# Second attention: exponentials over 1536 columns out of two score buffers of three banks, sums of every seventh tile on ScalarE

## What is computed

```python
q, k, v = jnp.split(x_proj, 3, axis=-1)
att = jnp.einsum('blhd,bmhd->blmh', q, k) * scale
att = jax.nn.softmax(att, axis=2)
opt = jnp.einsum('blmh,blhd->blhd', att, v).reshape(b, l, d)
...
x = x + _L1_attn_ref(xn, ...) + _L1_ffn_ref(xn, ...)   # second layer
```

## Time and profile before

| | |
|---|---|
| Time, median of 3 runs | 1465.37 us (1465.34 to 1466.09) |
| Time of the profiled execution | 1468.72 us |
| Its span, first to last instruction | 1467.0 us |
| ScalarE busy | 1428.0 us |
| VectorE busy | 1220.8 us |
| TensorE busy | 1110.7 us |
| GpSimd busy | 884.5 us |
| First exponential of the second attention | 975.7 us |

### The profile page before, as it was taken

The page is one execution under the profiler, slowest core; times in us unless marked ns, Lnnn a source line. Parts: engine busy times, 40 slices in busy tenths (PEclk is TensorE's granted clock), DMA queues, the critical chain, the costliest instruction groups (busy, mean ns, idle before and its releaser), DMA issues.

```text
span 1467.0 us, 22437 instructions
## 1 busy us (share of the span) xinstructions
PE 1110.7 (76%) x8231; PEld 445.9 (30%) x8260; DVE 1220.8 (83%) x2196; ACT 1428.0 (97%) x796; POOL 884.5 (60%) x656
## 2 busy tenths in 40 slices
PE   5587787888788888888887675777777677776766
PEld 2133224245143352452542311322223122221212
DVE  6998889978879879789788588838898898998886
ACT  3999999999999999999999999989999999999998
POOL 5188998878789898898898985933213023022100
PEclk8599988999999999899999897889999999999999
DMA  4942544222322235254353231034033033021020
GB/s 121 253 141 65 167 129 125 60 61 73 82 82 62 64 102 155 80 144 131 83 155 96 69 75 31 13 120 81 27 128 71 27 113 81 27 106 33 23 70 20
DMA packets 113185, 130.04 MB, mean 89 GB/s; under 512 B 42906, under 2 KB 81178, under 8 KB 113066
## 3 DMA queue, kind: packets, MB, share of 16 engines
q1 hardware_dynamic: 107738, 116.74, 29.5%
q0 software_dynamic: 4464, 11.09, 2.8%
q10 hardware_dynamic: 864, 0.69, 0.2%
HBM read 83.79 MB, written 44.70 MB: 88 GB/s over the span
## 4 chain that ended last, share of the span: by engine, by line
ACT 38%; POOL 27%; DVE 15%; issue 12%; PE 6%; DMA 2%; SPq 1%; ACTq 0%; DVEq 0%; POOLq 0%
ACT exp L1352 13%; ACT scores L830 11%; ACT scores L791 6%; DVE exp L1360 6%; DVE scores L737 6%; POOL scratch L775 3%; POOL scores L773 3%; ACT exp L1348 3%; PE pvb L718 3%; POOL gate L1098 3%; POOL scratch L784 3%; POOL scores L786 3%; POOL scratch L780 3%; ACT h L1091 2%; POOL scratch L777 1%
## 5 line engine op out<-in xcount | busy, mean ns | idle before, releaser
L737 DVE TENSOR_SCALAR scores<-ring 128x1024 f32<-128x1024 f32 x512 | 591.8, 1216 | 62.2 <-PE ring L703 58.9
L830 ACT ACTIVATE scores<-scores 128x8192 f32<-128x8192 f32 x63 | 438.9, 7020 | 0.2
L1352 ACT ACTIVATE exp<-ring 128x1024 f32<-128x1024 f32 x438 | 431.4, 1388 | 4.4 <-PE ring L1327 3.9
L718 PE MATMUL pvb<-scores,val 128*9 128x256 f32 x4096 | 338.3, 406 | 97.8 <-ACT scores L830 63.7
L1327 PE MATMUL ring<-stk 128*128 128x512 bf16 x995 | 300.9, 386 | 131.2 <-ACT exp L1352 103.4
L791 ACT ACTIVATE scores<-scores 128x7296 f32<-128x7296 f32 (+2 forms) x59 | 384.1, 6574 | 4.9 <-DVE scores L737 4.8
L1360 DVE SCALAR_TENSOR_TENSOR exp<-exp 128x512 f32<-128x512 f32 x438 | 322.3, 758 | 62.6 <-ACT exp L1352 55.6
L703 PE MATMUL ring<-stk 64*128 64x512 bf16 x1024 | 216.1, 419 | 59.2 <-DVE scores L737 45.4
L1327 PEld LDWEIGHTS ring<-stk 128*128 128x128 bf16 x1024 | 66.1, 97 | 341.7 <-ACT exp L1352 232.5
L703 PEld LDWEIGHTS ring<-stk 64*128 64x128 bf16 x1024 | 50.0, 94 | 303.4 <-DVE scores L737 182.3
L718 PEld LDWEIGHTS pvb<-scores,val 128*9 128x9 f32 x4096 | 65.8, 89 | 226.9 <-issue 223.5
(11 more groups left out here) (263 smaller groups left out, 1434.9 us busy)
## 6 DMA issues: line engine op xcount, KB each, us to landing
stk<-stack SPq DMA_DIRECT2D x192, 192.0 KB, 2.8
w<-in_w SPq DMA_DIRECT2D x39, 352.0 KB, 3.6
w<-in_w SPq DMA_DIRECT2D x39, 192.0 KB, 2.7
stack<-qp SPq DMA_DIRECT2D x7, 768.0 KB, 4.4
stack<-kp SPq DMA_DIRECT2D x7, 768.0 KB, 5.4
xj<-xg SPq DMA_DIRECT2D x10, 448.0 KB
yg<-xj POOLq DMA_DIRECT2D x10, 448.0 KB, 3.6
stack<-qp SPq DMA_DIRECT2D x7, 512.0 KB, 5.1
```

What stands on the lines that cost most here:

```text
L718: mm = nc.tensor.matmul(pvb[place % 2][32 * c:32 * c + VW, 0:256], val[place][:, j, :], S[place][:, j * N + c * 256:j * N + (c + 1) * 256] ...
L737: nc.vector.tensor_scalar(S[place][:, j * N:(j + 1) * N], tile, 1e-12, None, ALU.max).then_inc(o.release(("qk", group, place, j)), 1)
L830: nc.scalar.activation(S[place][:], S[place][:], ACT.Exp, scale=-1.0).then_inc(exp_done, 1)
L1352: nc.scalar.activation(EX[k // 2][:, k % 2, :], tile, ACT.Exp, scale=SCALE1).then_inc(o.release(("qk1", n, i)), 1)
```

## The change

Scores go into two buffers of three banks, `wide0` and `wide1`, which take the place of `ring0` to `ring2` for the second attention; `widen` makes TensorE wait for all three old buffers first. Half tiles of 512 columns are counted through, and a span is a run of three of them (`SPAN_HALVES` = 3, 3, 3, 3, 2): four spans of one and a half tiles and one of a single tile, which holds tile 6 of a round of 7. That tile is summed on ScalarE in the first three batches; in the last batch VectorE sums all but the last 8 tiles. The first 504 tiles are cut in this way, the last 8 stay single. TensorE makes three matmuls for a wide span, ScalarE one exponential of 1536 columns; VectorE's sums remain one for each tile. `EX` is one tensor of 14 tiles used round and round, and the wait for the sums becomes one for each span, 14 tiles back. Because it is larger, the first exponential waits for the products of S[1] too. The auxiliary work stays at its steps; a span is filled at the step of its first tile, two spans ahead.

```diff
 def sum_by_act(n, i):
-    s = n % H * NT + i
-    return n < HEADS - H and 12 <= s < 124 and s % 5 == 1 or n >= HEADS - GROUP and i >= LAST_PARTS[-1][0]
+    return n < HEADS - H and (n * NT + i) % SPAN_TILES == SPAN_TILES - 1 or n >= HEADS - GROUP and i >= LAST_PARTS[-1][0]
...
+SPAN_HALVES, TILE_HALVES = (3, 3, 3, 3, 2), 2
+SPAN_TILES = sum(SPAN_HALVES) // TILE_HALVES
+EXP_TILES = 14
+LAST_SPANS = HEADS * NT - GROUP * (LAST_PARTS[-1][1] - LAST_PARTS[-1][0])
...
+for span_halves in LAST_SPANS // SPAN_TILES * SPAN_HALVES + (HEADS * NT - LAST_SPANS) * (TILE_HALVES,):
+    SPANS.append(range(len(SPAN_OF), len(SPAN_OF) + span_halves))
+    SPAN_OF.extend(span_halves * [len(SPANS) - 1])
...
+    def widen(self, pe, tiles):
+
+        for slot in range(RING):
+            pe.wait_ge(self.free[slot], self.turn[slot])
+        self.tiles, self.slot, self.slots = [*tiles, *self.tiles[len(tiles):]], 0, len(tiles)
...
-            EX = [late_room(f"exp{i}", [P, 2, N]) for i in range(NT // 2)]
+            EX = late_room("exp", [P, EXP_TILES * N])
...
+        with ExitStack() as own:
+            wide = [psum(own, f"wide{i}", [P, 3 * 512]) for i in range(2)]
...
+        def pe_scores1(pe, o, span):
+            tile = o.begin(pe, ("exp", span))
+            for k, half in enumerate(SPANS[span]):
+                (n, i), cols = tile_of(half), HALVES[half % TILE_HALVES]
+                if i == 0 and half % TILE_HALVES == 0:
+                    pe.wait_ge(stk1_in[n % GROUP], 16 * (n // GROUP + 1))
+                mm = nc.tensor.matmul(tile[:, k * 512:(k + 1) * 512], stk1[n % GROUP][:, Q, i * P:(i + 1) * P],
+                                      stk1[n % GROUP][:, K, cols], start=True, stop=True)
+            mm.then_inc(ring_full, 1)
+
+        def act_exp1(act, o, span):
+            halves = SPANS[span]
+            (n, i), last = tile_of(halves[0]), halves[-1] // TILE_HALVES
+            tile = o.filled(act, ("exp", span))
+            if span == 0:
+                act.wait_ge(pv_done, CHG * (GROUPS - 1) + 2 * CH)
+            if last >= EXP_TILES and FOLDS[last - EXP_TILES + 1]:
+                act.wait_ge(summed, FOLDS[last - EXP_TILES + 1])
...
         def dve_fold(dve, o, b, s):
-            (n, i), k = tile_at(b, s), s % NT
-            o.emptied(dve, ("qk1", n, i))
+            (n, i), half = tile_at(b, s), (b * H * NT + s) * TILE_HALVES
+            o.emptied(dve, ("exp", SPAN_OF[half + 1]))
...
-                for i in range(RING):
-                    pe_scores1(pe, o, 0, i)
+                o.widen(pe, [tile[:] for tile in wide])
+                made = len(wide)
+                for span in range(made):
+                    pe_scores1(pe, o, span)
...
-                        if b or s >= RING:
-                            pe_scores1(pe, o, *tile_at(b, s))
+                        while made < len(SPANS) and SPANS[made][0] // TILE_HALVES <= b * H * NT + s:
+                            pe_scores1(pe, o, made)
+                            made += 1
```

More of the change, by code:

```diff
@@ L205, in begin @@
         if slot is None:
-            slot, self.slot = self.slot, (self.slot + 1) % RING
+            slot, self.slot = self.slot, (self.slot + 1) % self.slots
         if self.turn[slot]:
@@ L210, in begin @@
         self.made[kind], self.turn[slot] = self.made[kind] + 1, self.turn[slot] + 1
-        self.of[key] = (kind, self.made[kind], slot, self.turn[slot])
+        self.of[key] = (kind, self.made[kind], slot, self.turn[slot], self.tiles[slot])
         return self.tiles[slot]
+    def widen(self, pe, tiles):
+        for slot in range(RING):
+            pe.wait_ge(self.free[slot], self.turn[slot])
+        self.tiles, self.slot, self.slots = [*tiles, *self.tiles[len(tiles):]], 0, len(tiles)
     def fills(self, key):
@@ L217, in filled @@
     def filled(self, eng, key):
-        kind, made, slot, _ = self.of[key]
+        kind, made, _, _, tile = self.of[key]
         eng.wait_ge(self.full[kind], made)
-        return self.tiles[slot]
+        return tile
     def release(self, key):
@@ L225, in emptied @@
     def emptied(self, eng, key):
-        _, _, slot, turn = self.of[key]
+        _, _, slot, turn, _ = self.of[key]
         eng.wait_ge(self.free[slot], turn)
@@ L1329, in scores1, with tile_of @@
             return mm
-        def pe_scores1(pe, o, n, i):
-            if i == 0:
-                pe.wait_ge(stk1_in[n % GROUP], 16 * (n // GROUP + 1))
-            tile = o.begin(pe, ("qk1", n, i))
-            scores1(tile, n % GROUP, i).then_inc(ring_full, 1)
-        def act_exp1(act, o, b, s):
-            (n, i), k = tile_at(b, s), s % NT
-            tile = o.filled(act, ("qk1", n, i))
-            if n:
-                if k % 2 == 0:
-                    act.wait_ge(summed, FOLDS[b * H * NT + s - NT + 2])
-            elif i == 0:
-                act.wait_ge(pv_done, CHG * (GROUPS - 1) + CH)
-            if sum_by_act(n, i):
+        def tile_of(half):
+            return tile_at(*divmod(half // TILE_HALVES, H * NT))
@@ new lines, in exp_cols @@
+        def exp_cols(half):
+            return half % (EXP_TILES * TILE_HALVES) * 512
+        def pe_scores1(pe, o, span):
[7 more added lines that the diff above has]
+            mm.then_inc(ring_full, 1)
@@ new lines, in act_exp1 @@
+        def act_exp1(act, o, span):
[6 more added lines that the diff above has]
+                act.wait_ge(summed, FOLDS[last - EXP_TILES + 1])
+            at_col = exp_cols(halves[0])
+            out, tile = EX[:, at_col:at_col + 512 * len(halves)], tile[:, 0:512 * len(halves)]
+            if len(halves) == TILE_HALVES and sum_by_act(n, i):
@@ L1346, in act_exp1 @@
                 if n >= 2 * GROUP:
                     act.wait_ge(w_done, n // GROUP - 1)
-                nc.scalar.activation(EX[k // 2][:, k % 2, :], tile, ACT.Exp, scale=SCALE1,
+                nc.scalar.activation(out, tile, ACT.Exp, scale=SCALE1,
                                      accum_out=den[n // GROUP % 2][:, n % GROUP, i:i + 1]
-                                     ).then_inc(o.release(("qk1", n, i)), 1)
+                                     ).then_inc(o.release(("exp", span)), 1)
@@ L1351, in act_exp1 @@
             else:
-                nc.scalar.activation(EX[k // 2][:, k % 2, :], tile, ACT.Exp, scale=SCALE1
-                                     ).then_inc(o.release(("qk1", n, i)), 1)
+                nc.scalar.activation(out, tile, ACT.Exp, scale=SCALE1).then_inc(o.release(("exp", span)), 1)
         def dve_fold(dve, o, b, s):
-            (n, i), k = tile_at(b, s), s % NT
-            o.emptied(dve, ("qk1", n, i))
+            (n, i), half = tile_at(b, s), (b * H * NT + s) * TILE_HALVES
+            o.emptied(dve, ("exp", SPAN_OF[half + 1]))
@@ L1358, in dve_fold @@
             if not sum_by_act(n, i):
-                tile = EX[k // 2]
+                at_col = exp_cols(half)
+                low, high = (EX[:, at_col + cols.start:at_col + cols.stop] for cols in HALVES)
                 nc.vector.scalar_tensor_tensor(
-                    out=tile[:, k % 2, 0:N // 2], in0=tile[:, k % 2, 0:N // 2], scalar=1.0,
-                    in1=tile[:, k % 2, N // 2:N], op0=ALU.mult, op1=ALU.add,
+                    out=low, in0=low, scalar=1.0, in1=high, op0=ALU.mult, op1=ALU.add,
@@ L2023, in fast @@
                         act_exp0(act, r, place) if r or place else act_first_exp(act)
-                for b in range(B):
-                    for s in range(H * NT):
-                        if b == B - 1 and s == MAG_HEAD * NT:
-                            act_magnitudes(act)
-                        act_exp1(act, o, b, s)
+                for span in range(len(SPANS)):
+                    if span == SPAN_OF[MAG_TILE * TILE_HALVES]:
+                        act_magnitudes(act)
+                    act_exp1(act, o, span)
             by_guard(act, general, fast)
```

7 lines of the change are left out of this document (5 added, 2 removed).

## The result

Slower: 1476.14 us (median of 5, 1470.10 to 1478.49) against 1465.37 (median of 5 beside it), ratio 1.0067, interval 1.0054 to 1.0080. Run again twice it had 1472.29 (6 executions) and 1473.9 (4). The median of all 15 is 1473.7, 8.6 us over 1465.1 (28 executions of the kernel before on one chip), where the forecast had 3.4. Its executions spread over 9 us, those of the kernel before over 3 to 5 (but for one of 1485.9 us at a granted clock of 0.73 in place of 0.93).

A forecast was written before the change was run, and what follows sets the result against it. ScalarE's exponential chain was taken as the bound: 13.4 us of new waits against 10.1 gained, +3.3, +3.4 with rounding, gave 1468.8 us for the timed runs; range 1464.0 to 1472.5.

The forecast's parts named there:

- fixed costs and sums saved: ScalarE in the second attention: 144 fixed costs of 0.063 us and 12 sums go, gain 10.1 us.
- rounds: Each round's wide exponential behind the narrow one gets its scores late by 0.02 or 0.10 us; 2.7 us in all.
- bias products: Six TensorE products of 1.72 us between score fills delay ScalarE, 4.9 us against 0.8 before; 4.1 us.
- value projection and mixes: TensorE standing for VectorE handshakes: 2.1 us at line 1287, 1.4 at 1272, 0.3 at the projections; 3.7 us.
- behind the magnitudes: After the four magnitudes TensorE is at its 1.2 GHz clock, a fill 0.65 us longer; two waits, 1.1 us.
- first fill: At the stage's start, at the lower clock, ScalarE waits for three matmuls of 0.43 us each; 0.4 us.
- tail: Last 8 tiles: bias and products of part 0 cost 0.9 us; a later product of part 1 delays the end 0.5 us.
- The walk of TensorE's order: Stepping through TensorE's program with traced durations to find ScalarE's waits at bias products, projections and mixes: 4.1 and 3.7 us.
- the section on the lower clock: Charged TensorE's 1.2 GHz clock only behind the four magnitudes (1.1 us) and at the stage's first fill (0.4 us).
- The rival with the larger fixed cost: ScalarE's fixed cost per exponential is 0.094 us or more, so 4.5 us better, 1464.3 us; chance 14%.
- VectorE became no bound: Rival: 12 more sums leave ScalarE waiting for room in the 14 tiles, 1472.5 us; chance 6%.
- The waits were not ridden over: Rival: TensorE's chunks fall in its idle time, only the rounds' 2.7 us stay, 1458.0 us; chance 6%.

The follow-up runs named there:

- the split and the moves: changed kernel with each bias product given in two halves (1470.9 us); then also value projection at step 99 and mixing at 111 and 121 (1468.8 us).
- after_hold: changed kernel with only GpSimd's gathers for the second block held back until the sum of tile 30; 1472.3 us, ratio 1.0038.
- gather_late: changed kernel with halved bias products, moved steps, unused products, last output projection one step later, GpSimd's gathers held back; 1463.4 us, ratio 0.9991.
- tail_again: changed kernel with halved bias products, moved steps, unused products and last output projection one step later, gathers not held, second run; 1464.6 us, ratio 1.0001.
- gather_late4: fourth run of the kernel with halved bias products, moved steps, unused products, later last projection and gathers held back; 1464.5 us, ratio 0.9984.
- the narrow kernels: changed kernel's 14 tiles and sums of every seventh, but exponentials of 1024 columns: three buffers 1467.0 us (1.0015), two buffers 1474.7 us (1.0065).
- narrow_two: changed kernel's 14 tiles and sums of every seventh, but exponentials of 1024 columns from two buffers of two banks; 1474.7 us, ratio 1.0065.

## Why the prediction was wrong

The direction was right, the size was not: +8.6 for +3.4, beyond the upper end of 1472.5. Point by point:

| step | forecast us | shown in the profile after |
|---|---|---|
| fixed costs and sums saved | -10.1 | -10.1: wide exponentials 1.343 us apart, narrow ones 0.917 (medians), 62 sums |
| rounds | 2.7 | 3.8, with all other waits under 0.2 and one of 0.3 |
| bias products | 4.1 | 4.4, less 1.2 that three buffers pay there: 3.2 |
| value projection and mixes | 3.7 | 0.58, 0.96 and 0.75, 0.92, 0.42: 3.6 |
| behind the magnitudes | 1.1 | 0.32, 0.75, 0.23: 1.3 |
| first fill | 0.4 | 0.88 us from its load to the exponential at the full clock, where two matmuls take 0.66: 0.2 |
| tail | 0.9, 0.5 | 1.18 less 0.26: 0.9; behind the last exponential 5.94 less 5.31: 0.6 |
| lower clock elsewhere | none | 3.2, and 2.1, 7.7, 4.1 in three more profiles |
| late release | none | 0, and 0 and 1.7 in two more; in six of all twelve profiles 2.5 on average |

The walk of TensorE's order was good to some tenths at each of its places, and to 1.1 us in the rounds, so what it says of *where* waits come is shown: the split and the moves took them away where they changed the order. "Before, three buffers hid it; now only 0.32 us" was right as well, but for 0.2 us at each bias product, and I then counted what is larger than 0.32 us only among TensorE's jobs in its program. **The step that failed** is the list of what the lost buffer uncovers: the section on the lower clock had it behind the magnitudes and at the first fill alone. A fill of three at that clock is 0.65 us longer by the forecast's own numbers, twice what is to spare, and after the change the clock falls in the stage itself, three to nine times an execution, each for 0.5 to 1.6 us of waits: 4.3 us in the mean of four profiles (three of the changed kernel and `after_hold`), where the forecast had nothing. The late release, of which it could know nothing, adds 1.2 (six in twelve, 2.5 each). The forecast's own terms as measured are right in sum: 12.8 of waits (3.8 + 3.2 + 3.6 + 1.3 + 0.9), 0.2 at the first fill and 0.6 at the end, less 10.1, which is 3.5 for 3.4.

Together that is 1465.1 + 3.5 + 4.3 + 1.2 = 1474.1, where 1473.7 was measured. That it comes so close is partly luck. The same sum for each of the four profiled executions gives 1471.8, 1470.7, 1478.0 and 1472.7, and they took 1470.1, 1470.9, 1474.7 and 1472.3: the start of the first exponential (972.9 to 975.3) and the stretch behind the magnitudes vary as well, and four profiles are few.

The rival with the larger fixed cost fell: exponentials out of the score buffers stand 1.34 us apart, so 0.063 fixed. By the figures of the Trainium skill ("ScalarE: Activation LUTs", section "What ACT_TABLE_LOAD costs") an estimate is 1.37 apart; this trace has 1.34. VectorE became no bound: ScalarE has no wait for the sums in any row of the waits. The waits were not ridden over. That rival's condition, new waits under 7.2 us, was just met in the profiles of `gather_late` and `tail_again` (8.6 less the 1.5 of three buffers), and their times are 0.1% under and level with the kernel before, not clearly faster.

**Best version.** `gather_late` to `gather_late4` is one kernel, 46 executions: medians 1463.4 to 1464.5, ratios 0.9982 to 0.9991, two of the four intervals below 1. It is 1.3 to 2.6 us faster than the kernel before by these ratios, 0.1 to 0.2%, which is hardly more than nothing, and 10 us faster than the changed one.

**Open.** What holds TensorE's completions at that one place; why the clock falls in the wide kernel and at other steps in each execution; and what the executions at 1475 us and above of the changed kernel with the unused products spend, as only one of these was profiled (1477.25 us: late release 3.1, clock 3.4, step 3 1.9).

## What to carry to other kernels

Work out what the chain between two uses of a buffer has to spare (here 0.32 us with two; with three, by the same working, about one exponential more), and then hold against it everything that can lengthen a fill: each piece of other work, and TensorE at its lower clock, which can return inside a steady stage, as here, though it needn't (the narrow kernels had none). A third buffer buys insurance whose price is known and whose worth varies from execution to execution. Cutting long pieces in two, shifting pieces off the short exponentials, and unused products brought the kernel back level with the one before; of the 10.1 us that the wider instruction saves, 1.3 to 2.6 were left at best. Before cutting a piece in two, see that a fill stands between the halves.

## What the runs showed that I had not expected

- The granted clock fell inside a steady stage of the changed kernel, at steps that differ from execution to execution (three to nine stretches in each of four profiles between the first tiles and the end), while the same stage with 1024 columns a fill, on two buffers or three, had none except at the first tiles and behind the magnitudes. How busy TensorE is doesn't tell them apart: from 1400 to 1440 us it is busy for 25.5 us in the changed kernel, where the clock fell, and for 26.0 in the kernel before and 26.3 in `narrow_two`, where it didn't. Unused products that took it to 36 us in these 40 kept the clock up.
- ScalarE stood for up to 3.2 us for matmuls that should have ended, and two more engines with it, at one place of the program, in six of twelve profiles, and in none of five in which GpSimd's gathers stood elsewhere. Where they stood near it, a shift of 0.4 to 0.65 us against TensorE's work went with it in all eleven wide profiles.
- The third score buffer is worth 7.75 us of 1467 at 1024 columns, with almost no spread in `narrow_two` (1474.6 to 1476.0), whereas the wide kernel on two buffers spreads over 9 us: what varied was the price of the clock and of the late release, and the start of the stage by 3.4 us.
